# Cross-attention and a mixture of experts on one core: output projection with tokens on the partitions, the experts' second bias as one split product, the first pair's row sums behind the second pair's scores

## The chip, the core and the metric

The kernel runs on one core of a Trainium2 chip. The metric is the device time of one execution in microseconds. TensorE (PE) multiplies, VectorE (DVE), ScalarE (ACT) and GpSimd (POOL) work on the results, and SyncE (SP) issues the loads and stores.

## What is computed

x is (4, 256, 128), the context (4, 1601, 96), all in float32; 8 heads of 64; 8 experts of width 256 of which each token takes 2, and one shared expert.

```python
def attention(x, context, Wq, Wk, Wv, Wo, bo):
    q, k, v = heads(x @ Wq), heads(context @ Wk), heads(context @ Wv)
    attn = softmax(einsum('bhsd,bhld->bhsl', q, k) * 64 ** -0.5)
    return merge(einsum('bhsl,bhld->bhsd', attn, v)) @ Wo + bo

def experts(hidden, router_w, router_b, sw1, sb1, sw2, sb2, rw1, rb1, rw2, rb2):
    probs = softmax(hidden @ router_w + router_b)
    weights = top-2 of probs, zero elsewhere
    shared = gelu(hidden @ sw1 + sb1) @ sw2 + sb2
    h1 = gelu(einsum('td,edh->teh', hidden, rw1) + rb1)
    mixed = einsum('ted,te->td', einsum('teh,ehd->ted', h1, rw2) + rb2, weights)
    return shared + mixed

x = x + attention(layernorm(x), context, ...)
x = x + experts(layernorm(x), ...)
```

## The kernel before

**Work.** The attention goes by batch b (4) and pair of heads p (4), 16 pairs in all, written (b, p). Wq and Wk are multiplied ahead of time into `m`; a pair's `g` is m times the normalised x, 96 rows by 2 heads x 256 tokens. Keys are cut into 13 chunks of 128 (the last has 65), and two chunks make a unit u, so units 0 to 6. For each chunk `scores` multiplies the context by g into one of three PSUM banks (lines 1149 to 1151), and ScalarE writes the exponentials into one of 7 slots of `probs` (line 754). `values` (line 1165) multiplies the probabilities by v; all values of a pair follow all its scores. The softmax's shift comes from 16 `max` products per pair (line 1079, one 402-key block, 128 tokens and one head each), which VectorE reduces (line 880), and whose result is transposed (`shift`, line 1085) and copied into a 97th row of g (line 888).

**Split products.** Most products are of numbers split into a high and a low part of a type that TensorE multiplies in one record: three products stand for one. The sums, values, output projection and the experts' second bias are plain float32 products, which the trace shows as two records each.

**Sums of the softmax.** The sum over keys is first made over units: GpSimd adds unit after unit into `work` (lines 525 and 527, 128 x 1024), VectorE adds the last unit and the two halves (lines 529 and 530), and `sums` (line 1033) multiplies the outcome by ones. `quotient` divides the values by it (lines 828 and 830). A semaphore `summed` counts the additions. ScalarE writes a slot of `probs` again only when the values and the sum of the unit that was in it are done.

**Context.** Each batch's context is split in four pieces (`ctx`): ScalarE takes the high part (line 693), GpSimd the low part (line 618, 96 x 402), one batch ahead.

**After a batch.** `y` is the output projection (line 1090), with channels on the partitions; VectorE adds the bias bo and copies it to `yT` (line 891); `yt` transposes it (line 1095), VectorE adds x and takes the moments (lines 814, 817, 820, 821), GpSimd makes the inverse roots (lines 602, 603), ScalarE normalises (`norm`, line 699), `xt` transposes it for the router and the experts. The expert stage follows the last pair; its second layer begins with the product of the weights of the experts with the second biases (line 1210).

**Order.** `plan` writes one list of steps from the table of costs `PE_US` and `DVE_US`; every engine runs through this list and takes its part, so an engine's queue is in that order. Small steps that share four PSUM banks are of kind `ring`. The main list holds scores, values, sums and what stands at fixed places (`behind`: at unit u, so many pairs after the pair's end; `ctx` pieces at units 1 to 4 of p == 0 of the batch before). The tasks of the next pair (maxima, g, the layer norms of x) are put in between where the model of the engines' times finds room.

## Time and profile before

| | us |
|---|---|
| median of 3 runs (lowest, highest) | 456.32 (454.98, 456.7) |
| profiled execution, its own time | 456.58 |
| its span, first to last instruction | 454.8 |
| TensorE busy | 440.4 |
| VectorE busy | 299.7 |
| GpSimd busy | 251.1 |
| ScalarE busy | 218.5 |

The mean granted TensorE clock is 0.992 of full speed. Busy time of TensorE is what the trace counts for matrix products, of which it models the ends; weight loads overlap them and are counted apart. The time outside the span, 1.8 us, is start and end.

### The profile page before, as it was taken

The page shows a single profiled execution, that of the slowest core. Times are in us where ns is not written, and L with a number is a line of the kernel's source. Part 1 is how long each engine was busy: PE and PEld are TensorE (multiplying, and loading weights), DVE is VectorE, ACT ScalarE, POOL GpSimd, SP SyncE. Part 2 cuts the span into 40 slices and gives each one's busy share as a digit, 9 for nine tenths or more (in the row PEclk, how much of TensorE's full clock was granted, in tenths as well). Part 3 has the DMA queues.
Part 4 walks back from the last instruction along what each step waited for, and adds up shares of the span by engine and source line. Part 5 has one row for each costly group of instructions (what it writes and reads, how often), then busy time and mean ns, then how long its engine had stood idle before and what let it go on. Part 6 is the DMA issues. An engine that isn't in the chain of part 4 may idle for free. (4 is left out here: it accounts for less than half of the span.)

```text
span 454.8 us, 7273 instructions
## 1 busy us (share of the span) xinstructions
PE 440.4 (97%) x2565; PEld 337.4 (74%) x2565; DVE 299.7 (66%) x587; ACT 218.5 (48%) x384; POOL 251.1 (55%) x167
## 2 busy tenths in 40 slices
PE   9998799999999999999999999999999999999996
PEld 7875677777786868687867686778777766777885
DVE  4694676877536969594448788854468676648443
ACT  3563252423581425253733443427625745687673
POOL 5969182928192555472853747454616540567772
PEclk9999699999999999999999999999999999999999
DMA  7400100000002000000030000000000000000000
GB/s 229 113 1 1 54 3 0 1 1 0 2 0 56 0 1 2 0 1 2 0 105 0 1 0 2 0 2 1 1 1 1 0 1 1 1 1 0 25 2 23
DMA packets 5194, 7.27 MB, mean 16 GB/s; under 512 B 644, under 2 KB 4136, under 8 KB 5160
## 3 DMA queue, kind: packets, MB, share of 16 engines
q1 hardware_dynamic: 5160, 6.81, 5.1%
q8 instruction: 22, 0.36, 0.3%
q14 instruction: 12, 0.10, 0.1%
HBM read 6.29 MB, written 0.52 MB: 15 GB/s over the span
## 5 line engine op out<-in xcount | busy, mean ns | idle before, releaser
L754 ACT ACTIVATE probs<-ps 128x512 f32<-128x512 f32 (+1 forms) x208 | 123.6, 597 | 171.6 <-PE ps L1151 165.4
L880 DVE TENSOR_REDUCE maxes<-ps 128x1 f32<-128x402 f32 x256 | 132.9, 567 | 46.0 <-PE ps L1079 45.5
L527 POOL TENSOR_TENSOR work<-work,probs 128x1024 f32<-128x1024 f32 x54 | 128.6, 2382 | 12.2 <-ACT probs L754 9.8
L525 POOL TENSOR_TENSOR work<-probs 128x1024 f32<-128x1024 f32 x14 | 33.5, 2391 | 126.9 <-issue 115.3
L1165 PE MATMUL ps<-probs,v_sb 128*64 128x256 f32 (+1 forms) x832 | 93.4, 381 | 0.0
L1149 PE MATMUL ps<-g_hi,ctxT_hi 97*128 97x512 f32 (+1 forms) x208 | 84.2, 405 | 0.2 <-DVE g_hi L888 0.2
L1165 PEld LDWEIGHTS ps<-probs,v_sb 128*64 128x64 f32 (+1 forms) x832 | 58.4, 137 | 33.6 <-issue 4.1
L1150 PE MATMUL ps<-g_lo,ctxT_hi 96*128 96x512 f32 (+1 forms) x208 | 82.5, 397 | 0.0
L1151 PE MATMUL ps<-g_hi,ctxT_lo 96*128 96x512 f32 (+1 forms) x208 | 82.2, 395 | 0.0
L1079 PE MATMUL ps<-ctxT_hi,g_hi 96*128 96x402 f32 x256 | 78.3, 370 | 3.6 <-issue 2.2
L1079 PEld LDWEIGHTS ps<-ctxT_hi,g_hi 96*128 96x128 f32 x256 | 47.4, 192 | 19.6 <-issue 5.9
L678 POOL TENSOR_TENSOR g_lo<-probs,g_hi 128x512 fp32r<-128x512 f32 x32 | 40.7, 1291 | 35.6 <-ACT g_hi L776 34.3
L1151 PEld LDWEIGHTS ps<-g_hi,ctxT_lo 96*128 96x128 f32 (+1 forms) x208 | 39.0, 187 | 10.2
L1149 PEld LDWEIGHTS ps<-g_hi,ctxT_hi 97*128 97x128 f32 (+1 forms) x208 | 38.7, 186 | 6.8 <-DVE g_hi L888 0.9
L1150 PEld LDWEIGHTS ps<-g_lo,ctxT_hi 96*128 96x128 f32 (+1 forms) x208 | 39.2, 188 | 3.6
L828 DVE RECIPROCAL rden<-ps 128x128 f32<-128x128 f32 x32 | 30.3, 948 | 7.4 <-PE ps L1033 7.4
L963 DVE TENSOR_TENSOR probs<-ps,probs 128x512 f32<-128x512 f32 x32 | 20.6, 685 | 20.7 <-PE ps L1121 14.5
L732 ACT COPY v_sb<-ps 128x512 f32<-128x512 f32 (+1 forms) x39 | 22.8, 585 | 22.5 <-PE ps L993 19.8
L791 ACT ACTIVATE probs<-ps,biasT 128x512 f32<-128x512 f32 x36 | 24.6, 688 | 17.3 <-PE ps L993 15.7
L529 DVE TENSOR_TENSOR work<-work 128x512 f32<-128x512 f32 x16 | 11.5, 718 | 31.0 <-POOL work L527 30.7
L991 PE MATMUL ps<-wv_hi,ctxT_hi 96*128 96x512 f32 (+1 forms) x52 | 21.1, 406 | 0.1
L776 ACT CAST g_hi<-probs 128x512 fp32r<-128x512 f32 x36 | 20.3, 616 | 0.4 <-DVE probs L963 0.4
(145 smaller groups left out, 555.7 us busy)
## 6 DMA issues: line engine op xcount, KB each, us to landing
raw<-in_ctx_T_dram SPq DMA_DIRECT2D x3, 600.4 KB, 4.6
work<-in_L_ffn_rw_dram SPq DMA_DIRECT2D x1, 1024.0 KB, 7.7
raw<-in_ctx_T_dram SPq DMA_DIRECT2D x3, 150.8 KB, 2.6
x_sb<-in_x_dram SPq DMA_DIRECT2D x1, 384.0 KB, 6.5
early<-in_WqkT_dram SPq DMA_DIRECT2D x1, 336.0 KB, 5.1
wo_sb<-in_L_xattn_Wo_dram SPq DMA_DIRECT2D x1, 256.0 KB, 5.7
out_dram<-x_sb SPq DMA_DIRECT2D x1, 256.0 KB, 2.2
out_dram<-x_sb SPq DMA_DIRECT2D x2, 128.0 KB, 1.7
```

What stands on the lines that cost most here:

```text
L525: ops.tensor_tensor(acc, probs[:, (n - 1) % SLOTS], pr, ALU.add).then_inc(summed, 1)
L527: ops.tensor_tensor(acc, acc, pr, ALU.add).then_inc(summed, 1)
L678: g.tensor_tensor(hid_lo[:, w % SPLITS, :], activations(w), hid_hi[:, w % SPLITS, :].bitcast(F32), ALU.subtract).then_inc(hid_lo_ready, 1)
L754: nc.scalar.activation(probs[0:rows, n % SLOTS, j, :], s_bank(chunk_no(*w))[0:rows, :], ACT.Exp, scale=SCALE).then_inc(probs_ready, 1)
L791: nc.scalar.activation(hid[:, n % 4, :], ps[:, n % HB, :], ACT.Gelu, bias=biasT[:, c:c + 1]).then_inc(hid_ready, 1)
L828: v.reciprocal(rden[:, q], sums_bank[:, q]).then_inc(rden_ready, 1)
L880: v.tensor_reduce(maxes[:, p % 2, i * T + t, blk:blk + 1], src[:, 0:BW], AX.X, ALU.max).then_inc(ring_taken, 1)
L1079: ins = mm(dst[:, 0:BW], g_hi[0:C, b % 2, 2 * p + i, t * P:(t + 1) * P], ctxT_hi[0:C, b % 2, k0:k0 + BW], start=True, stop=True)
L1149: mm(dst, ctxT_hi[:, b % 2, ks], gh, start=True, stop=False)
L1150: mm(dst, ctxT_hi[0:C, b % 2, ks], gl, start=False, stop=False)
L1151: ins = mm(dst, ctxT_lo[:, b % 2, ks], gh[0:C], start=False, stop=True)
L1165: ins = mm(o_bank[DH * i:DH * (i + 1), :], v_sb[0:rows, c, h * DH:(h + 1) * DH], probs[0:rows, n % SLOTS, j, i * S:(i + 1) * S], start=(c ...
```

## The change

- The output projection's operands change places: eight products of 128 columns leave the tokens on the partitions, so `yT` and the step `yt` go. The bias bo is loaded on all partitions and added to x by GpSimd once, ahead of the first pair of batch 1.
- The experts' second bias becomes one product of the split type: the rows of `b2_parts` hold high parts twice and low parts, and `wrow` holds the high weights twice.
- The first pair's `sums` stand behind the scores of unit 3 of the second pair, its quotients at unit 4, and all its additions are GpSimd's.
- The context pieces are taken at p == 1 instead of p == 0.
- The moments' two small last operations go from VectorE to GpSimd, where the sign is put right after the product.
- `g` of a pair stands in the middle of the maxima of the pair before, `y` at unit 2, and the model holds a pair's maxima until its g is split.

```diff
-PE_US = {"scores": 0.7, "v": 0.7, "values": 0.43, "max": 0.19, "g": 0.71, "shift": 0.44, "sums": 0.43, "y": 1.75,
-         "yt": 0.22, "xt": 0.22, "xn": 0.5, "router": 1.35, "wrow": 0.44}
-DVE_US = {"max": 0.51, "g": 1.45, "shift": 0.72, "y": 0.5, "yt": 1.8, "xt": 0.95,
-          "xn": 1.5, "router": 0.5, "rank": 2.6, "wrow": 0.7, "stats": 1.3, "quotient": 1.2, "add": 1.2}
+PE_US = {"scores": 0.7, "v": 0.7, "values": 0.43, "max": 0.19, "g": 0.71, "shift": 0.44, "sums": 0.43, "y": 1.9,
+         "xt": 0.22, "xn": 0.5, "router": 1.35, "wrow": 0.44}
+DVE_US = {"max": 0.51, "g": 1.45, "shift": 0.72, "y": 1.4, "xt": 0.95,
+          "xn": 1.5, "router": 0.5, "rank": 2.6, "wrow": 0.7, "stats": 1.0, "quotient": 1.2, "add": 1.2}
...
-            put.update({3: ("normal", 1), 5: ("normal", 2), 7: ("normal", 3), 9: ("xn", 0), 11: ("xn", 1)})
+            put.update({2: ("normal", 1), 4: ("normal", 2), 6: ("normal", 3), 9: ("xn", 0), 11: ("xn", 1)})
         if n and n + 1 < len(order):
-            put[len(maxima) - 3] = ("g",) + order[n + 1]
+            put[len(maxima) // 2 - 1] = ("g",) + order[n + 1]
...
-    behind = {(1, 2): [("ring", ("y",))], (3, 2): [("ring", ("yt",))], (5, 2): [("norm",)],
+    behind = {(2, 2): [("ring", ("y",))], (5, 2): [("norm",)],
...
-                if n and u < 2 and j == 1:
-                    main.append(("quotient", order[n - 1] + (u,)))
-            if p == 0 and b + 1 < batches and 0 < u <= blocks:
+                if n and (u, j) in (((4, 0), (4, 1)) if n == 1 else ((0, 1), (1, 1))):
+                    main.append(("quotient", order[n - 1] + ((u, j) in ((4, 1), (1, 1)),)))
+            if (n, u) == (1, 3):
+                main.append(("sums", order[0]))
+            if p == 1 and b + 1 < batches and 0 < u <= blocks:
...
-        main += held + [("sums", (b, p))] * (n + 1 < len(order))
+        main += held + [("sums", (b, p))] * (0 < n < len(order) - 1)
...
+        if name == "g":
+            g_end[w[1:3]] = dve - DVE_US["g"] / 2 + HOP_US
...
+                if task[0] == "max":
+                    at = max(at, g_end.get(task[1:3], 0.0))
...
-            5: [("ring", ("router", last)), ("exp", last)], 6: [("rank", last), ("best", last)], 8: [("ring", ("wrow", last))]}
-    behind = {2: [("ring", ("yt", b))], 3: [("norm", b)]}
+            5: [("ring", ("router", last)), ("exp", last)], 6: [("rank", last)], 7: [("best", last)], 8: [("ring", ("wrow", last))]}
+    behind = {3: [("norm", b)]}
...
+        def twice(rows):
+
+            return rows.rearrange("p t (a r) -> p t a r", r=W3)
+
+        def high_weights(rows):
+
+            return (twice(rows)[:, :, :, 0:E], w_hi[:].bitcast(F32).unsqueeze(2).to_broadcast([P, TH, P // W3, E]))
...
         def adds(pair, u):
 
+            if pair == 0:
+                return "pool"
...
-            sp.dma_start(bias_rows[NE * HK:NE * HK + 1], bo.rearrange("(k p) -> k p", p=P)).then_inc(s_bias, 16)
+            sp.dma_start(bo_sb[:], bo.rearrange("(o d) -> o d", o=1).to_broadcast([P, D])).then_inc(s_bo, 16)
...
-            sp.dma_start(b2_rows[E:E + 1], sb2.rearrange("(o d) -> o d", o=1)).then_inc(s_b2, 16)
+            sp.dma_start(b2_rows[W3:W3 + E], rb2).then_inc(s_b2, 16)
+            for r in (0, W3):
+                sp.dma_start(b2_rows[r + E:r + E + 1], sb2.rearrange("(o d) -> o d", o=1)).then_inc(s_b2, 16)
...
+                then_own(g.tensor_scalar(veps[:, tiles], mv[:, tiles, 1], LN_EPS, None, ALU.add))
                 then_own(g.tensor_tensor(rstd[:, tiles], veps[:, tiles], neg_half[:, tiles], ALU.pow))
-                g.tensor_tensor(shift[:, tiles], mv[:, tiles, 0], rstd[:, tiles], ALU.mult).then_inc(rstd_ready, 1)
+                then_own(g.tensor_tensor(shift[:, tiles], mv[:, tiles, 0], rstd[:, tiles], ALU.mult))
+                g.tensor_scalar(shift[:, tiles], shift[:, tiles], -1.0, None, ALU.mult).then_inc(rstd_ready, 1)
...
-            g.memset(wrow[:, :, E:E + 1], 1.0).then_inc(wrow_zero, 1)
+            g.memset(twice(wrow)[:, :, :, E], 1.0).then_inc(wrow_zero, 1)
...
-                    g.tensor_copy(wr[:, :, 0:E], hi)
+                    g.tensor_copy(*high_weights(wr))
                     g.tensor_tensor(wr[:, :, WLO:WLO + E], weight[:], hi, ALU.subtract).then_inc(w_ready, 1)
+                if kind == "scores" and w == (1, 0, 0, 0):
+
+                    pool.wait_ge(xn_ready, B - 1)
+                    pool.wait_ge(s_bo, 16)
+                    g.tensor_tensor(x_sb[:], x_sb[:], bo_sb[:].unsqueeze(1).to_broadcast([P, NT, D]), ALU.add
+                                    ).then_inc(bo_added, 1)
+                if kind == "scores" and w == (2, 1, 0, 0):
+                    pool.wait_ge(s_b2, 80)
+                    then_own(g.tensor_copy(b2_parts[:], b2_rows[:]))
+                    low_rows = b2_parts[W3:P, :]
+                    g.tensor_tensor(low_rows, b2_rows[W3:P, :], low_rows.bitcast(F32), ALU.subtract
+                                    ).then_inc(b2_split, 1)
+                    pool.wait_ge(b2_split, 1)
...
-                if kind == "ring" and w[0] == "yt":
+                if kind == "ring" and w[0] == "y":
...
-                then_own(ins)
-                ts = slice(tiles[0], tiles[-1] + 1)
-                v.tensor_scalar(mv[:, ts, 0], mv[:, ts, 0], -1.0, None, ALU.mult)
-                v.tensor_scalar(veps[:, ts], mv[:, ts, 1], LN_EPS, None, ALU.add).then_inc(var_ready, 1)
+                return ins
...
-                if kind == "values" and w[2:] == (0, 0):
+                if kind == "values" and w[2:] == (0, 0) and w[:2] != (0, 0):
...
-                        v.tensor_scalar(yT[:], src[:, 0:S], biasT[:, NE * HK:NE * HK + 1], None,
-                                        ALU.add).then_inc(ring_taken, 1)
-                    elif w[0] == "yt":
-
+
+                        dve.wait_ge(bo_added, 1)
                         tiles = range(b * T, (b + 1) * T)
                         v.tensor_tensor(x1[:, b * T:(b + 1) * T, :], src[:, 0:T * D].rearrange("p (t d) -> p t d", t=T),
                                         x_sb[:, b * T:(b + 1) * T, :], ALU.add).then_inc(ring_taken, 1)
                         dve.wait_ge(*taken(w))
-                        moments(x1, tiles)
+                        moments(x1, tiles).then_inc(var_ready, 1)
...
-                        for c in range(PAIRS):
-                            ins = mm(dst[:, 0:S], wo_sb[:, c, :], oT[:, b % 2, c, :], start=(c == 0),
-                                     stop=(c == PAIRS - 1))
-                    elif w[0] == "yt":
-                        pe.wait_ge(*taken(("y", b)))
                         for t in range(T):
-                            ins = turn(dst[:, t * D:(t + 1) * D], yT[:, t * P:(t + 1) * P], idr)
+                            for c in range(PAIRS):
+                                ins = mm(dst[:, t * D:(t + 1) * D], oT[:, b % 2, c, t * P:(t + 1) * P], wo_sb[:, c, :],
+                                         start=(c == 0), stop=(c == PAIRS - 1))
...
-                        mm(acc, b2_rows[:], wT[:, q].bitcast(F32), start=True, stop=False)
+                        mm(acc, b2_parts[:], wT[:, q], start=True, stop=False)
```

**TensorE's queue around the end of the first pair.** Rows give the line, the result and the operands, and the shape. Before, the row sums (`work,ones`) and the shift (`neg_max`) follow the values (`probs,v_sb`):

```order
L1079 MATMUL ps<-ctxT_hi,g_hi 128x402
L1165 MATMUL ps<-probs,v_sb 64x256 x26
L1033 MATMUL ps<-work,ones 64x256 x2
L1085 MATMUL ps<-ident,neg_max 97x128 x4
L1079 MATMUL ps<-ctxT_hi,g_hi 128x402 x3
L1149 MATMUL ps<-g_hi,ctxT_hi 128x512
```

In the changed kernel the shift stands ahead of the values, and behind them are maxima, a g and the second pair's first scores:

```order
L1116 MATMUL ps<-ident,neg_max 97x128 x4
L1110 MATMUL ps<-ctxT_hi,g_hi 128x402 x2
L1193 MATMUL ps<-probs,v_sb 64x256 x26
L1110 MATMUL ps<-ctxT_hi,g_hi 128x402 x3
L1022 MATMUL ps<-xnT_hi,m 96x256
L1023 MATMUL ps<-xnT_lo,m 96x256
L1024 MATMUL ps<-xnT_hi,m 96x256
L1022 MATMUL ps<-xnT_hi,m 96x256
L1023 MATMUL ps<-xnT_lo,m 96x256
L1024 MATMUL ps<-xnT_hi,m 96x256
L1110 MATMUL ps<-ctxT_hi,g_hi 128x402 x2
L1177 MATMUL ps<-g_hi,ctxT_hi 128x512
```

The row sums have moved behind the eighth score chunk of the second pair, where the changed kernel has:

```order
L1177 MATMUL ps<-g_hi,ctxT_hi 128x512
L1178 MATMUL ps<-g_lo,ctxT_hi 128x512
L1179 MATMUL ps<-g_hi,ctxT_lo 128x512
L1064 MATMUL ps<-work,ones 64x256 x2
L1110 MATMUL ps<-ctxT_hi,g_hi 128x402 x3
```

**GpSimd's queue in the first and second pair.** Before, from the first pair's first sum (`work<-probs`) to the second pair's; the pieces of the context are `ctxT_lo`:

```order
L525 TENSOR_TENSOR work<-probs 128x1024
L618 TENSOR_TENSOR ctxT_lo<-raw,ctxT_hi 96x402
L527 TENSOR_TENSOR work<-work,probs 128x1024
L602 TENSOR_TENSOR rstd<-veps,neg_half 128x2
L603 TENSOR_TENSOR shift<-mv,rstd 128x2
L618 TENSOR_TENSOR ctxT_lo<-raw,ctxT_hi 96x402
L527 TENSOR_TENSOR work<-work,probs 128x1024
L618 TENSOR_TENSOR ctxT_lo<-raw,ctxT_hi 96x402
L527 TENSOR_TENSOR work<-work,probs 128x1024
L618 TENSOR_TENSOR ctxT_lo<-raw,ctxT_hi 96x395
L527 TENSOR_TENSOR work<-work,probs 128x1024
L525 TENSOR_TENSOR work<-probs 128x1024
```

In the changed kernel, from the first pair's second sum:

```order
L545 TENSOR_TENSOR work<-work,probs 128x1024 x4
L547 TENSOR_TENSOR work<-work 128x512
L548 TENSOR_TENSOR work<-work,probs 65x512
L543 TENSOR_TENSOR work<-probs 128x1024
L640 TENSOR_TENSOR ctxT_lo<-raw,ctxT_hi 96x402
L545 TENSOR_TENSOR work<-work,probs 128x1024
L640 TENSOR_TENSOR ctxT_lo<-raw,ctxT_hi 96x402
L545 TENSOR_TENSOR work<-work,probs 128x1024
L640 TENSOR_TENSOR ctxT_lo<-raw,ctxT_hi 96x402
L545 TENSOR_TENSOR work<-work,probs 128x1024
L640 TENSOR_TENSOR ctxT_lo<-raw,ctxT_hi 96x395
L545 TENSOR_TENSOR work<-work,probs 128x1024
```

The first pair's sums are in one piece and end with VectorE's two additions, and the four pieces of the context stand between the second pair's sums.

## Rows read from the trace of the kernel before

**Rows 1.** The page, busy time and the clock by slices of 11.4 us.

```profile
PE 440.4 (97%) x2565; PEld 337.4 (74%) x2565; DVE 299.7 (66%) x587; ACT 218.5 (48%) x384; POOL 251.1 (55%) x167
...
PEclk9999699999999999999999999999999999999999
```

**Rows 2.** TensorE's waits: engine, line, who ended them, total us, times, longest.

```profile
PE ps L1033 <- DVE work L530: 4.8, 2, 4.0
...
PE ps L1079 <- DVE maxes L880: 1.0, 2, 0.7
```

**Rows 3.** The timeline around the first boundary: start, us, engine, line, operands, idle before.

```profile
38.63 5.84 PE L1165 MATMUL ps<-probs,v_sb 128*64 128x256 f32 x52
...
48.44 0.66 PE L1033 MATMUL ps<-work,ones 128*64 128x256 f32 x4 [3.97 <-DVE work L530]
```

**Rows 4.** Windows: stretch, its length, TensorE busy, granted clock, DMA share, GB/s.

```profile
44.47:48.44 3.97, 0.00 (x0) 1.00 0.56 155
...
49.00:55.75 6.75, 6.75 (x21) 0.50 0.00 0
```

**Rows 5.** GpSimd's timeline, first and last of five sums of the first pair.

```profile
30.92 2.40 POOL L525 TENSOR_TENSOR work<-probs 128x1024 f32<-128x1024 f32 x1
...
44.60 2.33 POOL L527 TENSOR_TENSOR work<-work,probs 128x1024 f32<-128x1024 f32 x1
```

**Rows 6.** The second pair: GpSimd's five sums and TensorE's row sums.

```profile
58.54 2.38 POOL L525 TENSOR_TENSOR work<-probs 128x1024 f32<-128x1024 f32 x1 [11.60 <-ACT probs L754]
61.00 9.76 POOL L527 TENSOR_TENSOR work<-work,probs 128x1024 f32<-128x1024 f32 x4
...
72.27 0.65 PE L1033 MATMUL ps<-work,ones 128*64 128x256 f32 x4
```

**Rows 7.** GpSimd in pair (1, 0), first and last sum, four context pieces between.

```profile
123.42 2.40 POOL L525 TENSOR_TENSOR work<-probs 128x1024 f32<-128x1024 f32 x1 [10.77 <-issue]
...
136.94 2.39 POOL L527 TENSOR_TENSOR work<-work,probs 128x1024 f32<-128x1024 f32 x1
```

**Rows 8.** Pairs (1, 1) and (2, 1): GpSimd's first sum, roots, TensorE's row sums.

```profile
151.07 2.37 POOL L525 TENSOR_TENSOR work<-probs 128x1024 f32<-128x1024 f32 x1 [11.74 <-issue]
...
159.89 0.70 POOL L602 TENSOR_TENSOR rstd<-veps,neg_half 128x2 f32<-128x2 f32 x1 [0.18 <-DVE veps L821]
...
168.66 0.60 PE L1033 MATMUL ps<-work,ones 128*64 128x256 f32 x4
...
244.71 2.37 POOL L525 TENSOR_TENSOR work<-probs 128x1024 f32<-128x1024 f32 x1 [11.26 <-issue]
...
262.23 0.60 PE L1033 MATMUL ps<-work,ones 128*64 128x256 f32 x4
```

**Rows 9.** TensorE's timeline: a maximum, a score chunk's first record, two maxima.

```profile
84.31 0.34 PE L1079 MATMUL ps<-ctxT_hi,g_hi 96*128 96x402 f32 x1
84.49 0.39 PE L1149 MATMUL ps<-g_hi,ctxT_hi 97*128 97x512 f32 x1
...
85.18 0.52 PE L1079 MATMUL ps<-ctxT_hi,g_hi 96*128 96x402 f32 x2
```

**Rows 10.** The chain that ended last: projection, bias product, four transposes.

```profile
391.04 1.73 PE ps L1090 x8
392.77 0.86 PE ps L1210 x2
...
427.53 0.44 PE ps L1116 x4
```

**Rows 11.** The moments' small operations (ns, least, median, most), and one beside a sum.

```profile
L820 DVE TENSOR_SCALAR mv<-mv x8: 168/728/2303, 3.7 to 396.7; 128x2 f32<-128x2 f32 x8
...
L603 POOL TENSOR_TENSOR shift<-mv,rstd x7: 194/196/916, 28.5 to 397.8; 128x2 f32<-128x2 f32 x7
...
157.31 2.40 POOL L527 TENSOR_TENSOR work<-work,probs 128x1024 f32<-128x1024 f32 x1
...
158.02 1.73 DVE L820 TENSOR_SCALAR mv<-mv 128x2 f32<-128x2 f32 x1
```

More of the change, by code:

```diff
@@ L109, in plan @@
                     name = x[1][0] if x[0] == "ring" else x[0]
-                    if qp == pairs - 1 and name in ("y", "yt", "xt"):
+                    if qp == pairs - 1 and name in ("y", "xt"):
                         main.append(("ring", (name, qb)))
@@ L124, in plan @@
     pe = dve = act = 0.0
-    free, exp_end, max_end, shift_end = [0.0] * RING, {}, {}, {}
+    free, exp_end, max_end, shift_end, g_end = [0.0] * RING, {}, {}, {}, {}
     n_exp = 0
@@ L280, in build @@
     TH = HALF // P
-    WLO = 32
+    WLO, W3 = 32, 64
     assert D == P and 2 * DH == P and 0 < REST <= P and C + 1 <= P
@@ L358, in build @@
         oT = work[:, 1, :].rearrange("p (a b c) -> p a b c", a=2, b=PAIRS)
-        yT = sb("yT", [P, S])
-        bias_rows = sb("bias_rows", [NE * HK + 1, P])
-        biasT = sb("biasT", [P, NE * HK + 1])
+        bo_sb = sb("bo_sb", [P, D])
+        bias_rows = sb("bias_rows", [NE * HK, P])
+        biasT = sb("biasT", [P, NE * HK])
         w1_sb = work[:].rearrange("p a b -> p (a b)")[:, 0:NE * H].rearrange("p (e h) -> p e h", e=NE)
@@ L373, in build @@
         b2_rows = sb("b2_rows", [P, D])
+        b2_parts = sb("b2_parts", [P, D], F32R)
         select = sb("select", [P, E], F32R)
@@ L438, in build @@
         s_wo, s_bias, s_w1, s_w2 = sem("loaded_wo"), sem("loaded_bias"), sem("loaded_w1"), sem("loaded_w2")
-        s_rw, s_b2 = sem("loaded_router"), sem("loaded_b2")
+        s_rw, s_b2, s_bo = sem("loaded_router"), sem("loaded_b2"), sem("loaded_bo")
+        bo_added, b2_split = sem("bo_added"), sem("b2_split")
         pool_done = sem("pool_done")
@@ L832, in _ @@
             dve.wait_ge(s_x0, 16)
-            moments(x_sb, range(T))
+            then_own(moments(x_sb, range(T)))
+            v.tensor_scalar(veps[:, 0:T], mv[:, 0:T, 1], LN_EPS, None, ALU.add).then_inc(var_ready, 1)
             dve.wait_ge(rstd_ready, 1)
@@ L836, in _ @@
                 ins = v.tensor_scalar(xn[:, t, :], x_sb[:, t, :], mv[:, t, 0:1], rstd[:, t:t + 1],
-                                      ALU.add, ALU.mult)
+                                      ALU.subtract, ALU.mult)
             ins.then_inc(xn0_ready, 1)
@@ L866, in _ @@
                         if b == 1:
-                            v.tensor_copy(biasT[:], src[:, P * (t1 - t0):P * (t1 - t0) + NE * HK + 1]
+                            v.tensor_copy(biasT[:], src[:, P * (t1 - t0):P * (t1 - t0) + NE * HK]
                                           ).then_inc(s_bias_turned, 1)
@@ L947, in _ @@
                     wr = wrow[:, w * TH:(w + 1) * TH, :]
-                    v.tensor_copy(wr[:, :, 0:E], hi)
+                    v.tensor_copy(*high_weights(wr))
                     v.tensor_tensor(wr[:, :, WLO:WLO + E], weight[:], hi, ALU.subtract).then_inc(w_ready, 1)
@@ L951, in _ @@
                     dve.wait_ge(s_x, 16)
-                    moments(x_sb, range(w * T, w * T + T))
+                    moments(x_sb, range(w * T, w * T + T)).then_inc(var_ready, 1)
                 elif kind == "weigh":
@@ L1051, in _ @@
                         if b == 1:
-                            pe.wait_ge(s_bias, 48)
-                            nb = NE * HK + 1
+                            pe.wait_ge(s_bias, 32)
+                            nb = NE * HK
                             ins = turn(dst[:, (t1 - t0) * P:(t1 - t0) * P + nb], bias_rows[:, :], idr[0:nb, 0:nb])
@@ L1202, in _ @@
                         pe.wait_ge(*sums_done(*LAST_PAIR))
-                        pe.wait_ge(s_b2, 48)
+                        pe.wait_ge(b2_split, 1)
                         pe.wait_ge(w2_split, NE)
```

## The prediction

> **What bounds the kernel now.** The page first: TensorE is busy for 440.4 of 454.8 us, and its granted clock is full in every slice but one near 50 us [rows 1]. So only two things can change the time by much: work taken from TensorE, and the 14.4 us in which it stands idle together with the time in which its clock is low. The list of TensorE's waits names the largest by far: the row sums (line 1033) waited 4.8 us for VectorE's last addition (line 530), 4.0 us of it once [rows 2]. In the timeline the reader sees where: the first pair's value products start at 38.63 and end 5.84 us later, at 44.47; the row sums start at 48.44 [rows 3]. The windows add that TensorE did nothing for those 3.97 us, and that from 49.00 to 55.75 its granted clock was 0.50, that is 1.2 instead of 2.4 GHz, though it was busy all through [rows 4]. One stall is paid twice.
>
> Who is late there is GpSimd. In the first pair it sums the probabilities unit by unit from 30.92 to 46.93, with four pieces of the next batch's context between its sums [rows 5]; VectorE adds the last two. Behind the row sums stand, on TensorE's queue, the shift, the next maxima and all scores of the second pair.
>
> **The first boundary.** After the change the first pair's row sums stand behind the scores of unit 3 of the second pair. The second pair's scores begin near 46.7: 44.47, plus the shift and three maxima that now stand ahead of the values (0.9), three maxima, g and two maxima behind them (1.6), less 0.3 (below). Eight score chunks (5.6), six maxima (1.1) and six transposes of xn (0.6) later, near 54, the row sums are asked for (unit costs from [rows 9, 10]). GpSimd loses the four context pieces of that pair (0.9 each) and gains the last two additions, each half as wide as its 2.4 us sum, so 2.4 together, six small operations of the layer norms of 0.2, and up to 0.8 of waiting for the third statistics. It is done near 47.5: covered by 6 us. Exponentials of unit u in the second pair need the slot of `probs` of the first pair's unit u, so its values and its sum: the five sums end between 33 and 45, before their turn. So the 3.97 us go. The low clock goes with them: 6.75 us at half speed are 3.4 us of loss, less the 0.3 us that TensorE waited for the shift's copy inside; I take 3.1, between 2.8 and 3.4. Another 0.3 us of waiting for g just before goes too.
>
> **What comes back: the context pieces land in the second pair.** There the row sums still stand right behind the values, and GpSimd now has four more pieces before them. Before, GpSimd started at 58.54, ended its fifth sum at 70.76, and the row sums started at 72.27, 1.5 us later, behind VectorE's two additions: 13.7 us in all [rows 6]. TensorE's own work from the same point was nearly as long: from 0.9 us earlier, 9 score chunks of 0.70, 7 maxima of 0.18, three transposes, g (0.7) and the values (5.8) make 14.5, so 13.6. The two were level, with 0.1 to spare. With pieces between, as in the first pair of batch 1, GpSimd takes from 123.42 to 139.33, 15.9 us [rows 7]; with pieces of 0.9 as in the first pair it is 15.4 to 15.8. So the new chain is 15.4 to 15.9 + 1.5 = 16.9 to 17.4 us. TensorE's work after the change: 9 chunks 6.3, 12 maxima 2.2, shift 0.4, the moved row sums 0.4, values 5.8, together 15.1, less 0.9: 14.2. It will stand idle 2.7 to 3.2 us at the second boundary; I take 2.9. The stall moves one pair on and shrinks by 1 us.
>
> In batches 1 and 2 the same holds, softened by the output projection that lies in that pair. From GpSimd's first sum to the row sums it was 151.07 to 168.66 and 244.71 to 262.23, 17.6 us each [rows 8]. After: 15.4 to 15.9 + the inverse roots (0.95 in the rows, and two more operations of 0.2: 1.35) + 1.5 = 18.3 to 18.8. I take 1.0 us lost in each, 2.0 together (bounds 0.7 and 1.2 each). Batch 3 has no pieces, and in the first pairs of batches 1 and 2 nothing is won by their leaving: nine v products (6.3 us) lie in that stretch and make TensorE the later.
>
> **Output projection.** Now it is four products of 256 columns, 1.73 us, and two transposes, half of the 0.44 us that four take [rows 10]: 1.95. After: eight products of 128 columns, 16 records, each with a 128-column load of its own. The nearest row is those four transposes, four loads and four times 128 columns, 0.11 a record: 16 x 0.11 = 1.76, so -0.2. Upper bound: loads and columns don't overlap, 0.22 a record, 3.5 us, +1.6. I take -0.2, since the row has this very shape. In batches 0 and 1 it falls into the pairs that GpSimd now bounds and is worth nothing; batches 2 and 3 give -0.4. (Batch b is projected in the second pair of batch b + 1; the last one in the expert stage.)
>
> VectorE loses the copy to `yT` and, of each set of moments, lines 820 and 821. The first is worth a look: the same 128x2 operation took between 168 and 2303 ns, and where it took 1.73 us, from 158.02, it ended with the GpSimd sum that had begun at 157.31 [rows 11]. Freed, VectorE has up to a GpSimd sum (2.4 us) more in each pair with a projection. On GpSimd the like exists: line 603 took 916 ns once and 196 as a rule [rows 11], so two such operations more may cost 2 x 0.72 = 1.4 us beyond their 0.4. That is rival D below. The Trainium skill (Advanced Engine Details and Errata, VectorE Performance Modes) has a rule for it: VectorE's second SBUF port is shared with GpSimd, and instructions of the two can block each other. By that rule, with which line 820's row agrees, moving the pair of operations doesn't end the conflict but turns it round, and rival D would be the forecast.
>
> **The bias product.** In full precision it takes 0.86 us at 512 columns [rows 10] and half of that twice at 256. In the split type it is one record instead of two; three of that type and width are a score chunk of 0.70, so 0.23, and half of it at 256. Gain 0.63 + 2 x 0.31 = 1.25 us, in the expert stage. Its price is on GpSimd: a copy and a subtraction of 128 columns, under 1 us, and the bias bo added to all of x, one operation of the size of a sum, 2.4 us. Both stand ahead of the first sum of a pair, where GpSimd pauses for 10.8 to 11.7 us [rows 7, 8]; were that cover gone they would cost 3.4 us. SyncE's queue gets three loads more and a broadcast of bo, all before the context of batch 2, whose load in any case now waits for the second pair, and which is wanted 80 us later: nothing.
>
> **The new order.** g stands in the middle of the maxima, and maxima of the next pair wait in the plan until it is split. Maxima waited 1.0 us for VectorE [rows 2] and one row sum, in batch 2, 0.8 for line 530. I take -0.7 for all of this (bounds -2 and +0.5).
>
> **Sum**, against the profiled execution's own 456.58 us (span 454.8; the runs' median, 456.32, is 0.3 lower): -3.97 - 3.1 - 0.3 + 2.9 + 2.0 - 0.4 - 1.25 - 0.7 = -4.8, so 451.8 us.
>
> **Rivals.**
> (A) GpSimd keeps up in the second pairs: without the 4.9 us that I add, 446.9. Against it: before, the two were level to 0.1 us with no pieces at all.
> (B) The clock falls again, at the second boundary. The idle stretch of 3.97 us was followed by the low level; the next longest wait of the list, 4.8 less 4.0, was not [rows 1, 2]. Mine, 2.9, is nearer to the one that was. It would cost the same 3.1: 454.9.
> (C) Slower: the clock falls in the second pairs of all three batches. In batches 1 and 2 TensorE's work from GpSimd's first sum is 9 chunks 6.3, 11 maxima 2.0, g 0.7, shift 0.4, projection 1.8, values 5.8, less 0.9: 16.1 against a chain of 18.3 to 18.8, some 2.4 us of idle. If that is enough for the low level, it decides: 3 x 3.1 = 9.3 us more, 461.1.
> (D) GpSimd's small operations are held up, 1.4 us in each of the bound chains of batches 1 and 2: 454.6.
> (E) The change doesn't do what it says: exponentials of the second pair are held for slots, the three score banks fill, and TensorE stands and cools as before. Only the bias is won, 455.3. Against it: the first pair's five sums end before they are needed.
>
> **Chances and range.** Forecast 0.58, A 0.12, B 0.13, C 0.06, D 0.06, E 0.05. A measurement can tell this kernel from an unchanged one from about 0.5% on, 2.3 us: faster is below 454.0, slower above 458.6. The forecast's own range by its bounds is 450 to 454. Faster: forecast, A and a small part of B and D, 0.74; same: the rest of B and D, E and the forecast's edge, 0.19; slower: C and a remainder of B, 0.07. The range goes from 447.5, which leaves out most of A, to 455.2, which holds B and D and leaves out C and half of E.
>
> **What would show it.** In the new profile: TensorE busy without a gap from the first pair's values into the second pair's scores, and PEclk full at 50 us; then the row sums waiting for VectorE's last addition, some 3 us near 66, and about 2 us in the second pairs of batches 1 and 2; the projection's 16 records in 1.7 to 1.9 us; the bias product in one record. I am wrong if those waits are missing (A), if PEclk falls after them (B, C), if GpSimd's stretch there is above 19 us (D), or if the projection takes above 2.5 us.

## The result, and the profile after

The changed kernel takes 461.33 us in the median of 4 executions, the kernel before 455.89 us beside it: a ratio of 1.0112, 95% interval 1.0085 to 1.0138. It is slower by 1.1%, where 451.8 us had been forecast. In a later set of runs it took 460.31 us in the median of 12 against 456.56; the ratio given for that run, 1.0041 (1.0003 to 1.0078), leaves out four executions of 461.0 to 461.9 us as disturbed, since two others took 454.2.

The page and TensorE's waits of the changed kernel, to be held against [rows 1, 2]:

```profile
PE 441.4 (96%) x2586; PEld 341.8 (74%) x2586; DVE 290.5 (63%) x566; ACT 218.5 (48%) x384; POOL 259.6 (57%) x186
...
PEclk9999999999999988999999989999999999999999
...
PE ps L1064 <- DVE work L548: 8.1, 5, 2.7
PE ps L1022 <- POOL g_lo L713: 3.3, 4, 2.5
```

The one deep dip of the clock near 50 us is gone. There are two shallow ones instead, near 170 and 265 us, and the waits have grown: 8.1 us in five places for VectorE's last addition, where [rows 2] had 4.8 in two, and 3.3 us for GpSimd's splits, 2.5 of it in one place that is new. (`PE ps L1064 <- DVE work L548: 8.1, 5, 2.7` reads: line 1064 waited for line 548, 8.1 us in all, 5 times, 2.7 at the longest.) Windows show two more dips, which slices of 11.5 us even out (stretch, length, TensorE busy, granted clock, DMA share, GB/s):

```profile
49.00:55.00 6.00, 6.00 (x30) 1.00 0.02 4
112.00:114.00 2.00, 2.00 (x12) 0.78 0.00 0
114.00:116.00 2.00, 2.00 (x7) 0.50 0.00 0
116.00:118.00 2.00, 2.00 (x9) 0.86 0.00 0
168.00:174.60 6.60, 6.60 (x18) 0.50 0.01 1
263.00:267.00 4.00, 4.00 (x13) 0.57 0.33 111
400.00:402.00 2.00, 2.00 (x6) 0.50 0.00 0
402.00:404.00 2.00, 2.00 (x8) 0.68 0.00 0
```

The first window answers to [rows 4]: full clock, no gap. Length times missing clock over the other seven is 8.4 us, where [rows 4] gave 3.4. In front of each of the four low stretches TensorE had stood idle. The timeline shows three of these waits; the fourth, before the scores of pair (1, 0), has its own reading below.

```profile
167.42 0.85 PE L1064 MATMUL ps<-work,ones 128*64 128x256 f32 x4 [2.66 <-DVE work L548]
262.52 0.65 PE L1064 MATMUL ps<-work,ones 128*64 128x256 f32 x4 [2.14 <-DVE work L548]
399.65 0.64 PE L1022 MATMUL ps<-g_hi,w_hi 128*128 128x512 f32 x1 [2.54 <-POOL g_lo L713]
```

**Pairs (1, 1) and (2, 1).** GpSimd's first and last sum of (1, 1), and the first of (2, 1), beside [rows 8]:

```profile
148.50 2.38 POOL L543 TENSOR_TENSOR work<-probs 128x1024 f32<-128x1024 f32 x1 [11.38 <-issue]
...
163.55 2.37 POOL L545 TENSOR_TENSOR work<-work,probs 128x1024 f32<-128x1024 f32 x1
...
244.21 2.36 POOL L543 TENSOR_TENSOR work<-probs 128x1024 f32<-128x1024 f32 x1 [9.88 <-ACT probs L789]
```

From GpSimd's first sum to the row sums it is 167.42 - 148.50 = 18.9 and 262.52 - 244.21 = 18.3 us. Take the waits of 2.66 and 2.14 us off, and TensorE's own work is 16.3 and 16.2.

**Before pair (1, 0).** Nothing of this was forecast. GpSimd's addition of bo to x starts with VectorE's halving addition of pair (0, 3):

```profile
108.10 2.36 POOL L689 TENSOR_TENSOR x_sb<-x_sb,bo_sb 128x1024 f32<-128x1024 f32 x1
108.18 2.83 DVE L547 TENSOR_TENSOR work<-work 128x512 f32<-128x512 f32 x1 [2.53 <-POOL work L545]
...
111.79 0.65 PE L1064 MATMUL ps<-work,ones 128*64 128x256 f32 x4 [1.50 <-DVE work L548]
...
L547 DVE TENSOR_TENSOR work<-work x15: 687/693/2832, 66.9 to 382.5; 128x512 f32<-128x512 f32 x15
```

The last row (least, median, most, in ns) says that this addition takes 0.69 us as a rule; of the other fourteen only two took longer, 0.75 and 1.10. Here it takes 2.83 and ends 0.55 us after GpSimd's does (108.10 + 2.36 = 110.46), as if it had begun only then. The row sums wait 1.50 us for it.

**In the expert stage.** The last batch's inverse roots stand now at the place of `y` in GpSimd's list, no longer at that of `yt`. GpSimd waits there for VectorE's moments, with two splits of hidden values queued behind:

```profile
396.76 0.22 POOL L622 TENSOR_SCALAR veps<-mv 128x2 f32<-128x2 f32 x1 [2.73 <-DVE mv L852]
...
398.33 2.50 POOL L713 TENSOR_TENSOR g_lo<-probs,g_hi 128x512 fp32r<-128x512 f32 x2
```

**Projection and bias product**, beside [rows 10]:

```profile
391.91 1.95 PE L1122 MATMUL ps<-wo_sb,work 128*128 128x128 f32 x16
393.61 0.48 PE L1238 MATMUL ps<-m,b_parts 128*128 128x512 f32 x1
393.93 0.39 PE L1022 MATMUL ps<-g_hi,w_hi 128*128 128x512 f32 x1
```

Start to start the projection is 1.70 us for 16 records and the bias product 0.32.

**What the new order took away.** The waits of the maxima's products, first in the kernel before, then in the changed one; the last column is TensorE's idle time in front of them and what ended it:

```profile
L1079 PE MATMUL ps<-ctxT_hi,g_hi 96*128 96x402 f32 x256 | 78.3, 370 | 3.6 <-issue 2.2 <-DVE maxes L880 1.0 <-DVE g_hi L888 0.3
...
L1110 PE MATMUL ps<-ctxT_hi,g_hi 96*128 96x402 f32 x256 | 75.2, 367 | 0.4 <-DVE maxes L913 0.3
```

They have fallen from 3.6 to 0.4 us, the 2.2 us of short waits included for which the profile names no other engine ("issue").

### The profile page after: what moved, and what is told of

Same layout as the page of the kernel before. It is cut to its first block and busy times, and to the rows that moved or that the text cites. A ratio compares the mean times of both kernels' runs of the same rounds, so it can differ in the third digit from the quotient of the medians.

```text
span 458.8 us, 7317 instructions
## 1 busy us (share of the span) xinstructions
PE 441.4 (96%) x2586; PEld 341.8 (74%) x2586; DVE 290.5 (63%) x566; ACT 218.5 (48%) x384; POOL 259.6 (57%) x186
## 5 line engine op out<-in xcount | busy, mean ns | idle before, releaser
L1110 PE MATMUL ps<-ctxT_hi,g_hi 96*128 96x402 f32 x256 | 75.2, 367 | 0.4 <-DVE maxes L913 0.3
L547 DVE TENSOR_TENSOR work<-work 128x512 f32<-128x512 f32 x15 | 13.0, 866 | 29.9 <-POOL work L545 29.8
L1022 PE MATMUL ps<-g_hi,w_hi 128*128 128x256 f32 (+1 forms) x54 | 19.3, 358 | 3.5 <-POOL g_lo L713 3.3
L921 DVE CAST g_hi<-ps 1x512 fp32r<-1x512 f32 x16 | 11.1, 696 | 16.8 <-PE ps L1116 16.4
```

The source lines that it names most:

```text
L1022: mm(dst, a_hi, b_hi, start=start, stop=False)
L1110: ins = mm(dst[:, 0:BW], g_hi[0:C, b % 2, 2 * p + i, t * P:(t + 1) * P], ctxT_hi[0:C, b % 2, k0:k0 + BW], start=True, stop=True)
```

## The experiments

**Theory:** the time is lost at four places where TensorE waits 1.5 to 2.7 us, and paid again there as low clock: the context pieces lengthen GpSimd's chain in (1, 1) and (2, 1); the two additions of two SBUF operands hold each other up before (1, 0); the roots block the splits. **Rivals:** the low clock has a cause of its own; the long addition has another cause; the pieces cost as much wherever they stand.

### The bias addition behind VectorE's last addition

```diff
                     pool.wait_ge(s_bo, 16)
+                    pool.wait_ge(summed, PAIRS * (NU - 1))
                     g.tensor_tensor(x_sb[:], x_sb[:], bo_sb[:].unsqueeze(1).to_broadcast([P, NT, D]), ALU.add
```

> The changed kernel (461.3 us, 1.012 of before), in which GpSimd's addition of bo to x waits for VectorE's last addition of pair (0,3). Theory (two operations of two SBUF inputs each, on VectorE and GpSimd, hold each other up; the stall then lowers the clock): VectorE's line 547 there falls from 2.83 back to about 0.7 us, the row sums before pair (1,0)'s scores no longer wait 1.5 us, the clock stays full near 113 to 117 us; -1.5 -2.3 = -3.8, so about 457.5 us, 1.003 to 1.005 of before. Rival 1 (the long line 547 has another cause, such as a late fifth sum): it stays long, and the time stays at 461. Rival 2 (the stall goes, but the clock falls there anyway): -1.5, 459.8. Rival 3: the bias addition, now later, delays GpSimd's first sum of pair (1,0): a wait appears at that pair's row sums.

Measured: 457.70 us in the median of 12, ratio 0.9986 (0.9955 to 1.0018). Line 547 takes 0.69 us and the wait before (1, 0) is gone. The surprise is in the spread: five executions took 453.5 to 453.7 us at a mean clock of 0.995, seven 457.7 to 458.8 at 0.984 or 0.985. The profiled one is of the first kind. Its row sums of (1, 1), and the windows behind both waits:

```profile
165.12 0.65 PE L1065 MATMUL ps<-work,ones 128*64 128x256 f32 x4 [2.66 <-DVE work L548]
...
165.00:172.00 7.00, 6.88 (x36) 1.00 0.01 4
257.00:264.00 7.00, 6.84 (x36) 1.00 0.28 98
```

The same 2.66 us of waiting, and the clock stays full. So a stall of this length doesn't always lower the clock; whether it does differs between executions of one kernel. The stall's own 1.5 us and its clock can't be told apart in this median; a later run does that.

### The context pieces of batches 2 and 3 back in first pairs

```diff
-            if p == 1 and b + 1 < batches and 0 < u <= blocks:
+            if p == (0 if b else 1) and b + 1 < batches and 0 < u <= blocks:
```

> The changed kernel, in which the context pieces of batches 2 and 3 are split in the first pair of the batch before, as in the kernel before, and only batch 1's stay in the second pair. Theory (pieces lengthen GpSimd's chain of sums past TensorE's work, and each stall is paid again as low clock): the row sums of (1,1) and (2,1) wait 0.5 us at most instead of 2.66 and 2.14, the clock is full there; -2.66 -2.14 + up to 0.5 for the stall and -3.3 -1.7 for the clock: about -9, so 452.5 us, 0.990 to 0.994 of before. Rival 1 (the clock falls in those stretches whatever the stall): -4.5 only, 457. Rival 2 (the pieces cost as much in the first pairs, where nine v products and the exponentials also wait for ScalarE): the time stays within 1 us of 461.

Measured: 449.95 us, ratio 0.9843 (0.9815 to 0.9871). TensorE's waits for line 548 fall from 8.1 us in five places to

```profile
PE ps L1064 <- DVE work L548: 3.3, 3, 1.5
```

and its row sums of (1, 1) and (2, 1) don't wait at all. Against the changed kernel's 460.31 us in the next set of runs (the kernel before took 456.65 us here and 456.56 there) that is -10.4 us: 4.8 of stall, and 5.6 that go with the rise of the mean clock, in the profiled executions from 0.981 to 0.995. This alone makes the change a gain. The rival that the pieces cost as much in first pairs falls.

### The last roots behind the splits

```diff
-    behind = {3: [("norm", b)]}
+    behind = {2: [("roots", b)], 3: [("norm", b)]}
...
+                if kind == "roots":
+                    inverse_roots(slice(w * T, w * T + T), B + w + 1)
-                if kind == "ring" and w[0] == "y":
+                if kind == "ring" and w[0] == "y" and w[1] < B - 1:
```

> The changed kernel, in which only the last batch's inverse roots on GpSimd stand behind the splits of that turn of the expert stage, where they stood before the change. Theory (GpSimd waited 2.73 us for VectorE's moments with two splits of hid behind it, and the second products waited for those): TensorE's wait of 2.54 us for g_lo near 399.6 goes, and with it the low clock of 400 to 404 us, 1.7 us; -4.2, so about 457 us, 1.002 to 1.004 of before. Rival 1 (the roots now come late for the normalisation, and the transposes xt or the first products of the last experts wait): about as much comes back, 460 to 461. Rival 2 (stall goes, clock falls anyway): -2.5, 458.8.

Measured: 457.52 us, ratio 1.0019 (1.0000 to 1.0039), where about 457 was expected. Roots and splits have changed places, TensorE's wait for g_lo there is 0.20 us, and the clock behind it is full:

```profile
395.25 2.54 POOL L715 TENSOR_TENSOR g_lo<-probs,g_hi 128x512 fp32r<-128x512 f32 x2 [1.37 <-ACT g_hi L813]
397.87 0.22 POOL L622 TENSOR_SCALAR veps<-mv 128x2 f32<-128x2 f32 x1
...
396.00:404.00 8.00, 7.44 (x32) 1.00 0.00 0
```

### All three together

The edits are those above.

> The changed kernel with the three edits together: the bias addition behind VectorE's last addition, the pieces of batches 2 and 3 in first pairs, the last roots behind the splits. Theory (three separate places, each a stall and a low clock): the gains add, -3.8 -9 -4.2 = -17, 444.5 us, and somewhat less if clock loss remains behind the stall of pair (0,1): 444 to 447.5, 0.974 to 0.982 of before. Rival (the stalls share a cause, or another limit stands just behind them): the sum falls short by more than 3 us, above 448.

Measured: 444.99 us, ratio 0.9735 (0.9708 to 0.9763), all executions between 444.4 and 445.4. Against 460.31 us the three edits gave 2.6, 10.4 and 2.8 us one by one, 15.8 together; all at once they give 15.3. So the places are separate to within 0.5 us.

### The changed kernel once more

> The changed kernel once more, so that the three beside it stand against it on one chip. Its four executions so far lay within 1.1 us at a clock of 0.980 to 0.981. Expected 461 us, 1.008 to 1.014 of before. The kernel with the bias wait, whose stalls of 2.66 and 2.14 us are the same, ran in two groups (453.5 at a clock of 0.995 and 458 at 0.985): if the low clock after such a stall is a matter of chance, this one shows two groups too, some 4.6 us apart; if it hangs on what stands just before the stall, it shows one.

Measured: 460.31 us in the median; two executions at 454.2 us and a clock of 0.995, ten between 459.9 and 461.9 at 0.980 to 0.984. Two groups again, of unequal weight: what the clock does differs between executions, but the low kind is the rule. In its profiled execution the clock stayed full behind the wait of 1.48 us before (1, 0) and was low behind the other three.

### All context pieces in first pairs

```diff
-            if p == (0 if b else 1) and b + 1 < batches and 0 < u <= blocks:
+            if p == 0 and b + 1 < batches and 0 < u <= blocks:
```

> The kernel with all three edits (445.0 us), and batch 1's context pieces too in the first pair, as before the change. Theory: GpSimd then ends the first pair's sums 4 x 0.9 us later, at 51 instead of 47.5, still ahead of the row sums at 54.7, and its chain in the second pair falls from 16.7 us to about 13.2, below TensorE's 15; the waits of 1.17 us and of 0.62 us there go: 443.2 us, 0.968 to 0.972 of before. Rival (exponentials of the second pair wait for slots of probs, and TensorE for score banks, since the sums free them later): up to 3 us of new waits near 50, 446 to 448.

Measured: 443.25 us, ratio 0.9702 (0.9677 to 0.9726): the best kernel of the study, 3.0% under the one before. GpSimd's last operation of the first pair, and the clock:

```profile
50.22 1.28 POOL L548 TENSOR_TENSOR work<-work,probs 65x512 f32<-65x512 f32 x1
...
PEclk9999999999999999999999999999999999999999
```

GpSimd ends at 51.5, the row sums are asked for at 55.3. The pieces need not have moved at all. (The wait of 0.62 us near 62, expected to go, stays: that one is not theirs.)

### TensorE kept awake in the changed kernel

```diff
                 pair = b * PAIRS + p
+                for _ in range({(0, 3): 9, (1, 1): 17, (2, 1): 13}.get((b, p), 0)):
+                    mm(sums_bank[0:DH, 0:DH], ones[:], ones[:], start=True, stop=True)
                 pe.wait_ge(summed, (pair + 1) * (NU - 1))
...
+                    for _ in range(16 if n == 2 else 0):
+                        mm(sums_bank[0:DH, 0:DH], ones[:], ones[:], start=True, stop=True)
                     pe.wait_ge(hid_lo_ready, n + 1)
```

> The changed kernel with small products of ones (64 columns, 0.14 us each, into a bank that the row sums then overwrite) in front of the four waits after which the clock was low: 9 before the row sums of (0,3), 17 of (1,1), 13 of (2,1), 16 before the second product that waited for g_lo. The waits for VectorE and GpSimd stay as long. Theory (the idle time itself lets the clock fall): the clock stays full, and the 2.3 + 3.3 + 1.7 + 1.7 us of loss go: -8.5 to -9, with up to 0.3 us lost where the products run past the wait: 452.5 us, 0.990 to 0.994 of before. Rival (the low clock comes from something else, such as the load of the products before): the clock falls as before and the time stays at 461.

Measured: 453.76 us, ratio 0.9929 (0.9910 to 0.9949), six executions within 1.2 us at a clock of 0.999 or 1.0; 452.5 was expected. In pair (1, 1):

```profile
163.90 2.15 PE L1063 MATMUL ps<-ones 128*64 128x64 f32 x34
166.73 0.65 PE L1066 MATMUL ps<-work,ones 128*64 128x256 f32 x3 [0.69 <-DVE work L548]
```

The engine waits as long for VectorE, but not idle: 2.15 us of it are filled, and no slice shows a low clock. So without the idleness it doesn't fall, and in this kernel the fall cost 460.31 - 453.76 = 6.6 us.

### One operand instead of two in GpSimd's addition

```diff
-                    g.tensor_tensor(x_sb[:], x_sb[:], bo_sb[:].unsqueeze(1).to_broadcast([P, NT, D]), ALU.add
+                    g.tensor_scalar(x_sb[:], x_sb[:], 0.0, None, ALU.add
```

> The changed kernel, in which GpSimd's addition of bo to all of x is an addition of the constant zero to x: one operand from SBUF instead of two, same size, same place. The bias bo is left out of the output. Theory (the two engines hold each other up only where both read two operands from SBUF): VectorE's line 547 of pair (0,3), which lies beside it, takes 0.7 us instead of 2.83, and the kernel gains the 1.5 us of stall and 2.3 of clock: 457.5 us. Rival 1 (any GpSimd operation of that size holds VectorE's): 547 stays near 2.8 and the time at 461. Rival 2 (a one-operand operation on GpSimd has another length; if it is much shorter than 2.36 us the test says less).

This kernel leaves the bias bo out of its output.

Measured: 458.31 us, ratio 1.0023 (0.9998 to 1.0048). Neither theory nor rival:

```profile
108.78 2.78 POOL L689 TENSOR_SCALAR x_sb<-x_sb 128x1024 f32<-128x1024 f32 x1
...
108.85 1.51 DVE L547 TENSOR_TENSOR work<-work 128x512 f32<-128x512 f32 x1 [2.50 <-POOL work L545]
```

VectorE is held up, but for 0.8 us and not to the end of GpSimd's operation, which is the longer one here. The row sums wait 0.18 us.

### The first boundary of the kernel before, kept awake

```diff
                 pair = b * PAIRS + p
+                for _ in range(25 if pair == 0 else 0):
+                    mm(sums_bank[0:DH, 0:DH], ones[:], ones[:], start=True, stop=True)
```

> The kernel before, with 25 small products of ones (some 3.6 us) in front of the first pair's row sums, whose wait of 3.97 us for VectorE's last addition stays. It prices the low clock at that boundary by itself; the prediction took 3.1 us. Theory (the idle engine is what lets the clock fall): the clock is full from 48 to 56, the stall stays near 4 us, and the time falls by 1.5 (what the executions with a clock of 0.995 lose) to 5 us (those of 0.989), so the median by about 3.3: 453.3 us, 0.990 to 0.995, and the two or three groups of its executions become one. Rival (the low clock has another cause): no change, and the groups stay.

Measured: 454.41 us, ratio 0.9957 (0.9940 to 0.9974). The row sums still start at 48.35 (48.44 in [rows 3]), and the window of [rows 4] has a full clock:

```profile
49.00:55.75 6.75, 6.52 (x34) 1.00 0.00 0
```

The executions lie within 0.8 us, where those of the kernel before spread from 455.0 to 458.6. The low clock there costs 2.5 us in the median, not 3.1. The two timelines say the same: from the row sums to the same later score chunk it is 58.97 - 48.44 = 10.53 us in the kernel before and 56.24 - 48.35 = 7.89 here, 2.64 apart, where [rows 4] gives 3.4. The second score chunk of the second pair, what follows it and the later chunk, in the kernel before and then here:

```profile
53.45 0.63 PE L1149 MATMUL ps<-g_hi,ctxT_hi 97*128 97x512 f32 x1
...
54.73 0.87 PE L1079 MATMUL ps<-ctxT_hi,g_hi 96*128 96x402 f32 x2
...
58.97 0.50 PE L1149 MATMUL ps<-g_hi,ctxT_hi 97*128 97x512 f32 x1
...
50.40 0.51 PE L1151 MATMUL ps<-g_hi,ctxT_hi 97*128 97x512 f32 x1 [0.23 <-DVE g_hi L888]
...
51.78 0.40 PE L1151 MATMUL ps<-g_hi,ctxT_hi 97*128 97x512 f32 x1
...
52.47 0.53 PE L1081 MATMUL ps<-ctxT_hi,g_hi 96*128 96x402 f32 x2
...
56.24 0.50 PE L1151 MATMUL ps<-g_hi,ctxT_hi 97*128 97x512 f32 x1
```

At half the clock the second chunk took 1.28 us against 0.69, less than twice as long, and a wait of 0.23 us for the shift's copy, hidden before, is back.

### The bias product alone

The kernel before with the split product of the second bias and what it needs; no other part of the change.

> The kernel before, with the experts' second bias as one split product and nothing else of the change: copy and subtraction on GpSimd, three more loads, doubled weight rows. The prediction's term: -1.25 us, and nothing for what GpSimd does, so 455.3 us, 0.996 to 0.999 of before. Rival (GpSimd's small operations or the wider copies of the weights cost as much as the product gives): 456.6, 1.000.

Measured: 456.06 us against 456.89, ratio 0.9985 (0.9965 to 1.0004): -0.8 us, and no difference isn't excluded. The kernel before had no wait for VectorE's copy to `yT`; here, with the product shorter, there is one:

```profile
395.16 0.41 PE L1114 MATMUL ps<-ident,yT 128*128 128x128 f32 x2 [0.66 <-DVE yT L910]
```

From the projection's start to these transposes it is 4.16 us here and 4.14 in the kernel before, so at this place the shorter product gave nothing. In the changed kernel `yt` is gone and this wait can't arise; what the product gives there was not measured by itself.

### The first boundary alone

```diff
+            if (n, u) == (1, 3):
+                main.append(("sums", order[0]))
...
-        main += held + [("sums", (b, p))] * (n + 1 < len(order))
+        main += held + [("sums", (b, p))] * (0 < n < len(order) - 1)
...
+            if pair == 0:
+                return "pool"
```

(and the two quotients in unit 4, as in the change).

> The kernel before, with the row sums of the first pair behind unit 3 of the second pair's scores, its last additions on GpSimd, and its quotients in unit 4, and nothing else: the context pieces stay in first pairs. The prediction's terms for the first boundary are -3.97 for the stall and -3.1 for the clock, about -7, so 449.6 us, 0.982 to 0.988 of before. Theory (moving the context pieces was not needed for this): GpSimd ends the first pair's sums near 51, ahead of the row sums near 54, and there is no wait. Rival (with the pieces in the way GpSimd is late, and TensorE waits at the new place, or exponentials wait for slots): up to 3 us come back, 452 to 453, with a wait at the row sums near 54 or at score products near 50.

Measured: 450.44 us, ratio 0.9869 (0.9849 to 0.9890). That is 6.45 us of the 7.07 forecast for this boundary, with the pieces where they were: GpSimd ends at 50.6, and

```profile
56.08 0.65 PE L1037 MATMUL ps<-work,ones 128*64 128x256 f32 x4
```

has no wait. Against the kernel kept awake it is 454.41 - 450.44 = 4.0 us, the stall of [rows 3].

### The two additions beside each other in the best kernel

The best kernel without `pool.wait_ge(summed, PAIRS * (NU - 1))`.

> The best kernel so far (443.25 us: three edits and all context pieces in first pairs), with one of the edits taken back: GpSimd's addition of bo to x no longer waits for VectorE's last addition of pair (0,3). Theory (the two additions hold each other up): line 547 there takes 2.8 instead of 0.7 us, the row sums wait about 1.5 us, +1.5: 444.8 us if the clock stays full, up to 447 if it falls after that wait. Rival (the long line 547 of the changed kernel had to do with what else ran there): no wait and 443.3.

Measured: 445.03 us, ratio 0.9752 (0.9731 to 0.9774), 1.8 us more than with the wait, and the clock stays full there. (The two ran in different sets, in which the kernel before took 456.89 and 456.56 us, so 1.5 to 1.8 is what the medians say.)

```profile
106.75 2.36 POOL L689 TENSOR_TENSOR x_sb<-x_sb,bo_sb 128x1024 f32<-128x1024 f32 x1
...
106.83 2.83 DVE L547 TENSOR_TENSOR work<-work 128x512 f32<-128x512 f32 x1 [2.50 <-POOL work L545]
...
110.44 0.65 PE L1066 MATMUL ps<-work,ones 128*64 128x256 f32 x4 [1.48 <-DVE work L548]
```

The 2.83 us come again in another kernel at another time. The 1.48 us of waiting are its price without the clock, and the medians agree.

## Why the prediction was wrong

Two steps failed. The larger is the clock; the other is what GpSimd's operations do beside and behind others.

**The low clock after the change.** The forecast let the clock fall nowhere. It took the one stall of 3.97 us that was followed by the low level and one below 1 us that was not, and set the waits of 2 to 3 us that it had itself worked out on the harmless side; "the clock falls again" had 0.13 for one place and 0.06 for three. It fell at four places in one profile and at three in the other, after 1.5 to 2.7 us. Kept awake, the kernel is 6.6 us faster (460.31 to 453.76). That is most of the 9.5 us by which the forecast missed. Rival C had this mechanism, and its 461.1 is the time that came; it had two of the places, (1, 1) and (2, 1), and missed (0, 3) and the expert stage, while (0, 1), where it started, kept its clock. That its number fits is luck: it is 9.3 us of clock alone, and what came is 6.6 of clock and unforeseen stalls.

**"Both stand ahead of the first sum of a pair, where GpSimd pauses for 10.8 to 11.7 us."** True of GpSimd's time, and beside the point: that pause begins while VectorE makes the last additions of the pair before. The step asked only what waits for GpSimd, not what shares something with it. The bias addition was put at nothing and cost 1.5 us of stall before (1, 0), 1.5 to 1.8 in the medians at full clock. The prediction had even weighed the sharing rule, but for operations of 0.2 us (rival D) and not for the one of 2.4.

**The roots' place.** The step listed their two added operations and not that their anchor in the list moves from `yt` to `y`, ahead of two splits: 2.54 us of stall. Putting them back gave 2.8 us in the medians (460.31 to 457.52).

Term by term, the rest:

| Step | forecast | measured |
|---|---|---|
| Stall of the first boundary | -3.97 | -4.0 |
| Its low clock | -3.1 | -2.5 |
| New idle at the second boundary | +2.9 | +1.2, and +0.6 for ScalarE at 62 us |
| Its chain, and TensorE's own work beside it | 16.9 to 17.4; 14.2 | 16.7; 14.8 |
| Chain in (1, 1), (2, 1) | 18.3 to 18.8 | 18.9, 18.3 |
| TensorE's work there (from rival C) | 16.1 | 16.3, 16.2 |
| Projection | 1.76 | 1.70 |
| Bias product | -1.25 | -0.8, interval reaching 0 |
| The new order | -0.7, and -0.3 for g | not by itself; the maxima's waits fell by 3.2 |

The chains were right to 0.3 us; their difference to TensorE's work in (1, 1) and (2, 1), 2.2 to 2.7 us, stood in the prediction, but only as a rival's number. The sum charged 1.0 us a pair against the time before, which is right for the stall, and didn't ask what an idle stretch of over 2 us does to the clock. With every clock full the kernels stand at 454.41 before and 453.76 after, a gain of 0.65 (0.3 to 1.3, as one allows for the two sets of runs that they come from), where the sum without its clock term says 1.7. The unforeseen stalls (1.5 and 2.5) less what the second boundary came out shorter (1.1) would make it worse by 2.9, not by 1.1; so some 1.8 us were gained that the sum does not have. The waits in front of the maxima point to where: the sum takes 1.0 us for them and g together, and they fell by 3.2. The 2.2 us under "issue" it had left out, though they stand in the same list as [rows 2]. With the first boundary alone changed 1.8 of them remain, so they go with the rest of the change; that it is the new order was not tried by itself. (The 0.3 us of waiting for g "just before" the first boundary is a misreading: the two waits that the kernel before has for it, 0.23 and 0.28 us, lie at 74.32 and 255.50.)

Rivals A and E fell: GpSimd does not keep up, and the first boundary's stall is gone. D fell too: in (1, 1) and (2, 1) the roots' four operations take 0.20 to 0.72 us, none is held up.

## What to carry to other kernels

When work moves to an engine's quiet stretch, ask three things: who waits for that engine, who shares memory access with it in that stretch, and what stands behind the moved operation in its own queue if its input is late. Work out the idle time of TensorE itself, not only the difference to the time before: a wait of 2 us can be worth 2 us of stall and as much again of clock, in some executions and not in others. Where a wait can't be removed, small products in front of it are a cheap way to hold the clock, and to measure what it costs; and where a stall is cured by moving its consumer, as here, try that alone before moving the producer's other work.

## What the runs showed of the hardware

- Over the profiles of all kernels here, the 1.2 GHz level followed both of TensorE's stalls of 4.0 us, 13 of the 15 stalls of 2.1 to 2.7 us, 2 of the 5 of 1.45 to 1.52 us and none of the 8 of 1.16 to 1.19 us. Executions of one kernel differ in this: after the same 2.66 us the granted clock was 0.50 for 6.6 us in one kernel's profile and 1.00 in another's.
- A low stretch costs less than its length times the missing clock: 2.5 us where the windows give 3.4, and 6.6 where they give 8.4. In the first case a score chunk took 1.28 us at 1.2 GHz against 0.69 at 2.4, and 0.23 us of the stretch covered a wait that was there anyway; the rest of the difference was not traced.
- VectorE's addition of two SBUF operands beside GpSimd's of two took 2.83 us instead of 0.69 in each of the five kernels that ran the two side by side, and in the two whose rows are shown ended 0.55 us after GpSimd's. The Trainium skill (SBUF — State Buffer, SBUF: two separate sides) says that the two share a port pair as an exclusive lock for the whole instruction, and the loser fully blocks. By that rule, with which these rows agree, 547 had to wait for 110.46. Beside GpSimd's operation of one operand it took 1.51 us and ended 1.2 us ahead of it; there the trace does not show a lock for the whole instruction.
